# Macaron block on one core: exponentials over two PSUM banks, a shorter ring for score tiles, Q and K rows read by group

## The reference

```
x = x + 0.5 * ffn(layernorm(x))
x = x + attention(layernorm(x))
x = x + 0.5 * ffn(layernorm(x))

ffn(z):       probs = softmax(z @ router_w)                 # 8 experts, top 2 kept
              routed = sum_e combine[n, e] * (silu(z @ w1[e]) @ w2[e])
              shared = sigmoid(z @ shared_gate_w) * ((silu(gate) * up) @ shared_down)
attention(z): q, k, v = z @ Wq.T, z @ Wk.T, z @ Wv.T        # 16 heads of 8
              scores = q k^T / sqrt(8) - slope_h * (key - query), causal
              out = softmax(scores) v;  result = out @ Wo.T
```

## Time and profile before

| | |
|---|---|
| median of 3 runs | 333.55 us (333.43 to 335.55) |
| the profiled execution | 334.14 us |
| its span, first to last instruction | 331.5 us |
| TensorE busy | 287.5 us |
| VectorE busy | 253.2 us |
| ScalarE busy | 171.6 us |
| GpSimd busy | 124.5 us |
| mean granted TensorE clock | 0.958 |

### The profile page before, as it was taken

How to read it: one execution, slowest core, us unless ns; L and a number is a source line. 1 busy time by engine, 2 the same in 40 slices (tenths; PEclk the granted TensorE clock), 3 DMA queues, 4 the chain that set the end, 5 groups by cost and what they waited for, 6 DMA issues and landing times.

```text
span 331.5 us, 7083 instructions
## 1 busy us (share of the span) xinstructions
PE 287.5 (87%) x2328; PEld 186.1 (56%) x2328; DVE 253.2 (76%) x1061; ACT 171.6 (52%) x326; POOL 124.5 (38%) x253
## 2 busy tenths in 40 slices
PE   0498998989982899999899995998999999999995
PEld 0487887977650534334343343332344698889894
DVE  4559798788995488898788983899822397987865
ACT  2143332432350478877688874778688532424330
POOL 0466245306151044447414533384733342430300
PEclk9999999999996559999999998999899999999999
DMA  6810000690269002114702293000000000100010
GB/s 182 211 24 0 2 0 5 209 168 5 68 175 141 0 2 91 65 43 86 113 2 98 98 147 48 1 4 4 1 3 1 2 2 0 34 1 32 3 32 32
DMA packets 19899, 17.71 MB, mean 53 GB/s; under 512 B 1692, under 2 KB 18652, under 8 KB 19804
## 3 DMA queue, kind: packets, MB, share of 16 engines
q1 hardware_dynamic: 19144, 17.04, 23.3%
q10 hardware_dynamic: 720, 0.23, 0.3%
HBM read 9.74 MB, written 7.34 MB: 52 GB/s over the span
## 4 chain that ended last, share of the span: by engine, by line
PE 53%; DVE 16%; DMA 8%; POOL 7%; issue 6%; ACT 5%; SPq 4%; DVEq 0%; ACTq 0%; POOLq 0%
PE bank L837 13%; PE bank L968 8%; PE bank L936 7%; PE bank L775 6%; DMA QA<-smaxT 5%; DVE X L634 5%; PE bank L776 5%; PE bank L777 5%; DVE masked_s L702 3%; POOL probs L369 2%; ACT probs L479 2%; DVE stats L571 2%; DMA X<-in_x 2%; SPq L254 2%; PE bank L991 2%
## 5 line engine op out<-in xcount | busy, mean ns | idle before, releaser
L702 DVE CUSTOM_DVE_ANT_0 masked_s<-bank,causal_sb 128x512 f32<-128x512 f32 (+3 forms) x256 | 109.7, 485 | 23.9 <-PE bank L909 23.9
L479 ACT ACTIVATE probs<-bank 128x512 f32<-128x512 f32 x160 | 89.6, 602 | 39.5 <-PE bank L936 38.9
L634 DVE SCALAR_TENSOR_TENSOR X<-bank,coef,X 128x128 f32<-128x128 f32 x288 | 80.7, 342 | 21.0 <-PE bank L837 14.6
L837 PEld LDWEIGHTS bank<-w_sb,act 128*128 128x128 f32 x512 | 67.7, 193 | 5.9
L369 POOL TENSOR_SCALAR_AFFINE_SELECT probs<-probs 128x512 f32<-128x512 f32 x64 | 39.8, 636 | 79.5 <-ACT probs L479 79.5
L936 PE MATMUL bank<-QA,KA 57*128 57x128 bf16 (+3 forms) x256 | 59.3, 318 | 10.1 <-DMA QA<-smaxT 9.8
L837 PE MATMUL bank<-w_sb,act 128*128 128x128 f32 x512 | 67.9, 276 | 0.0
L909 PE MATMUL bank<-KA,QA 54*128 54x512 bf16 (+3 forms) x256 | 59.6, 320 | 6.9 <-DVE smax L702 6.0
L418 ACT ACTIVATE act<-bank 128x512 f32<-128x512 f32 x72 | 41.8, 594 | 40.1 <-PE bank L777 40.1
L968 PE MATMUL bank<-probs,VA 128*32 128x256 f32 (+2 forms) x640 | 53.4, 402 | 1.4 <-issue 0.9
L775 PE MATMUL bank<-XH,w_hi 128*128 128x512 f32 x88 | 42.8, 486 | 4.9 <-DVE gated L619 2.3
(11 more groups left out here) (83 smaller groups left out, 322.5 us busy)
## 6 DMA issues: line engine op xcount, KB each, us to landing
qk_scratch<-qk_parts SPq DMA_DIRECT2D x8, 384.0 KB, 2.6
QA<-qk_scratch SPq DMA_DIRECT2D x8, 384.0 KB, 6.1
KA<-qk_scratch SPq DMA_DIRECT2D x8, 384.0 KB, 9.5
qk_scratch<-qk_parts SPq DMA_DIRECT2D x8, 256.0 KB, 2.9
qk_scratch<-qk_parts SPq DMA_DIRECT2D x8, 128.0 KB, 2.8
QA<-smaxT SPq DMA_DIRECT2D x64, 3.0 KB
out_x<-X SPq DMA_DIRECT2D x4, 256.0 KB, 2.3
X<-in_x SPq DMA_DIRECT2D x3, 256.0 KB, 6.1
```

The source lines that it names most:

```text
L479: nc.scalar.activation(dst, src, ACT.Exp).then_inc(exp_done, 1)
L634: m = nc.vector.scalar_tensor_tensor(X[:, b * NT + t, :], Y_BANK[i % 3][:, t * P:(t + 1) * P], coef[:, j % 2, t, n:n + 1], X[:, b * NT + t ...
L702: r = nc.vector.tensor_tensor_reduce(masked_s[:, u % 4, off:off + n], bank[:, off:off + n], causal_sb[:, S - n:S], 1.0, -3e38, ALU.add, AL ...
L837: m = nc.tensor.matmul(Y_BANK[i % 3][:, r], a, w2_sb[:, n, :], start=True, stop=True)
```

## The change

Exponentials: banks 0 and 1 form one tensor (`wide0`), banks 3 and 4 another (`wide1`). Transposed units take four banks in turn, two for each pair of units; one ScalarE instruction handles a pair of units (1024 columns), once both are there, and TensorE waits at the first unit of a pair for the pair before the last. All counts of `exp_done` become counts of pairs.

Scores: bank 0 goes to the transposed units, so that score units keep the two banks 2 and 7 throughout, and TensorE waits for the scan of unit u-2.

Reads: `read_rows` takes a group in place of a batch, four DMAs of 96 KB. Those of batch 0 are issued at once as before. Those of batch 1 no longer stand ahead of `maximum_rows(0)`; group `n + 4` is read in step `n`, behind `maximum_rows(n + 1)`. TensorE waits for a group's rows at its first score unit.

```diff
--- before.py
+++ after.py
@@ -83,9 +83,14 @@
 
         scratch = nc.dram_tensor("qk_scratch", [2, B, P, 6, S], bf16, kind="Internal").ap()
 
-        banks = [ctx.enter_context(nc.psum_tensor(f"bank{i}", [P, S], f32)) for i in range(8)]
+        def psum(i, n):
+            return ctx.enter_context(nc.psum_tensor(f"bank{i}", [P, n * S], f32))
+
+        wide0, bank2, wide1 = psum(0, 2), psum(2, 1), psum(3, 2)
+        halves_of = lambda wide: [wide[:, k * S:(k + 1) * S] for k in range(2)]
+        banks = halves_of(wide0) + [bank2] + halves_of(wide1) + [psum(i, 1) for i in range(5, 8)]
         H_BANK, Y_BANK, M0, M1 = banks[0:2], banks[3:6], banks[6], banks[7]
-        T_BANK, O_BANK, MISC = [banks[3], banks[4], banks[1]], banks[5], banks[6]
+        T_BANK, T_WIDE, O_BANK, MISC = [banks[3], banks[4], banks[0], banks[1]], [wide1, wide0], banks[5], banks[6]
         ld_x = [sem(f"ld_x{b}") for b in range(B)]
@@ -108,7 +113,7 @@
         mid_qk, parts_ready = sem("mid_qk"), sem("parts_ready")
         v_ready, v_sb = sem("v_ready"), sem("v_sb")
         scr_q, scr_k = sem("scr_q"), sem("scr_k")
-        qa_ready, ka_ready = [sem("qa_ready0"), sem("qa_ready1")], [sem("ka_ready0"), sem("ka_ready1")]
+        rows_ready = [[sem(f"rows_ready{i}_{g}") for g in range(NG)] for i in range(2)]
         aot_ready, at_sb, wo_ready, x_att = sem("aot_ready"), sem("at_sb"), sem("wo_ready"), sem("x_att")
 
         s_ready, s_used = sem("s_ready"), sem("s_used")
@@ -142,7 +147,7 @@
 
         def score_bank(u):
 
-            return banks[(2, 7)[u % 2]] if u < EARLY else banks[(2, 7, 0)[(u - EARLY) % 3]]
+            return banks[(2, 7)[u % 2]]
 
         def early_scores(n):
 
@@ -180,7 +185,7 @@
 
         STEPS = range(0, NGT + 1)
         QK_SCALE = (float(HD) ** -0.5, 1.0)
-        XT_AT, READ_AT = {0: 2, 5: 3}, {4: 2, 8: 3}
+        XT_AT, VALUES_AT = {0: 2, 5: 3}, {4: 2, 8: 3}
 
         def projected_at(n, phase):
 
@@ -234,16 +239,18 @@
                     sp.dma_start(dst[:, 3:5, :], part[:, 0:2, :]).then_inc(scr_k, 16)
                     sp.dma_start(dst[:, 5, :], part[:, 0, :]).then_inc(scr_k, 16)
 
-            def read_rows(b):
-
+            def read_rows(G):
+
+                b, g = divmod(G, NG)
                 if b >= 2:
-                    sp.wait_ge(t_ready, NU * NG * (b - 1))
-                for i, (scr, to, ready) in enumerate(((scr_q, QA, qa_ready), (scr_k, KA, ka_ready))):
+                    sp.wait_ge(t_ready, NU * (G - 2 * NG + 1))
+                pairs = slice(GH // 2 * g, GH // 2 * (g + 1))
+                for i, (scr, to) in enumerate(((scr_q, QA), (scr_k, KA))):
                     sp.wait_ge(scr, 48 * (b + 1))
                     rows = scratch[i, b].rearrange("(pair par d) s n -> par d s pair n", par=2, d=HD)
                     for par in range(2):
-                        sp.dma_start(to[b % 2][64 * par:64 * par + PROD, :, :],
-                                     rows[par].rearrange("d s pair n -> (d s) pair n")).then_inc(ready[b % 2], 16)
+                        sp.dma_start(to[b % 2][64 * par:64 * par + PROD, pairs, :],
+                                     rows[par][:, :, pairs, :].rearrange("d s pair n -> (d s) pair n")).then_inc(rows_ready[b % 2][g], 16)
 
             def maximum_rows(G):
 
@@ -257,13 +264,15 @@
             for b in range(2):
                 write_parts(b, 0)
                 write_parts(b, 1)
-                read_rows(b)
+                if b == 0:
+                    for G in range(NG):
+                        read_rows(G)
             maximum_rows(0)
             for n in STEPS:
                 if 0 <= n + 1 < NGT:
                     maximum_rows(n + 1)
-                if n in READ_AT:
-                    read_rows(READ_AT[n])
+                if n + NG < NGT:
+                    read_rows(n + NG)
                 if (b := projected_at(n, 2)) is not None:
                     write_parts(b, 0)
                 if (b := projected_at(n, 3)) is not None:
@@ -363,7 +372,7 @@
 
             def mask(G, tiles):
                 for kt, need in tiles:
-                    pool.wait_ge(exp_done, NU * G + need)
+                    pool.wait_ge(exp_done, NU // 2 * G + need)
                     blk = probs[G % 2][:, :, POS[kt]:POS[kt] + P]
 
                     nc.gpsimd.affine_select(out=blk, in_=blk, compare_op=ALU.is_ge, fill=0.0, base=0,
@@ -372,12 +381,12 @@
             ffn(0)
             for n in STEPS:
                 if 0 <= n < NGT:
-                    mask(n, ((0, 4), (3, 8), (1, 8)))
+                    mask(n, ((0, 2), (3, 4), (1, 4)))
                 for k in range(2):
                     if (b := projected_at(n, 2 + k)) is not None:
                         low_qk(b, k)
                 if 0 <= n < NGT:
-                    mask(n, ((2, 10),))
+                    mask(n, ((2, 5),))
                 if 0 <= n + 2 < NGT:
                     split_smax(n + 2)
                 if n == LAST_LN:
@@ -462,20 +471,19 @@
                 nc.scalar.activation(VA[b % 2][:, :, :, 0:HD],
                                      M0[:, :].rearrange("p (t h d) -> p t h d", t=NT, d=HD), ACT.Copy).then_inc(v_sb, 1)
 
-            def exps(G, i):
-                u = NU * G + i
-                ac.wait_ge(t_ready, u + 1)
-                if i == 0 and G >= 2:
+            def exps(G, k):
+                u = NU // 2 * G + k
+                ac.wait_ge(t_ready, 2 * u + 2)
+                if k == 0 and G >= 2:
                     ac.wait_ge(pv_ready, G - 1)
-                a = prob_units(G % NG)[i]
-                head = a[0][1] - GH * (G % NG)
-                bank = T_BANK[u % 3]
-                if a[0][2] == 2:
-                    dst = probs[G % 2][:, head:head + 3:2, POS[2]:POS[2] + 2 * P]
-                    src = bank[:, :].rearrange("p (h n) -> p h n", h=2)
+                kt, src = prob_units(G % NG)[2 * k][0][2], T_WIDE[u % 2]
+                if kt == 2:
+                    dst = probs[G % 2][:, :, POS[2]:POS[2] + 2 * P].rearrange("p (h i) n -> p i h n", i=2)
+                    src = src[:, :].rearrange("p (i h n) -> p i h n", i=2, h=2)
                 else:
-                    pos = POS[a[0][2]]
-                    dst, src = probs[G % 2][:, head, pos:pos + S], bank[:, :]
+                    head = 2 * (k % 2)
+                    dst = probs[G % 2][:, head:head + 2, POS[kt]:POS[kt] + S]
+                    src = src[:, :].rearrange("p (i n) -> p i n", i=2)
                 nc.scalar.activation(dst, src, ACT.Exp).then_inc(exp_done, 1)
 
             def copy_smax(G):
@@ -517,8 +525,8 @@
             load_table(1, ACT.Exp)
             for n in STEPS:
                 for i in range(NU):
-                    if 0 <= n < NGT:
-                        exps(n, i)
+                    if 0 <= n < NGT and i % 2:
+                        exps(n, i // 2)
                     if (n, i) in VALUE_SLOTS:
                         values(VALUE_SLOTS.index((n, i)))
                     if i == 3 and 0 <= n + 1 < NGT:
...
@@ -894,13 +902,10 @@
                 if u == 0:
                     pe.wait_ge(ld_ac, 16 * 10)
                     pe.wait_ge(shift_ready, B)
-                if 2 <= u < EARLY + 2:
+                if u >= 2:
                     pe.wait_ge(s_used, u - 1)
-                elif u > EARLY + 2:
-                    pe.wait_ge(s_used, u - 2)
-                if i == 0 and g == 0:
-                    pe.wait_ge(qa_ready[b % 2], 32 * (b // 2 + 1))
-                    pe.wait_ge(ka_ready[b % 2], 32 * (b // 2 + 1))
+                if i == 0:
+                    pe.wait_ge(rows_ready[b % 2][g], 64 * (b // 2 + 1))
                 a, dst = score_units(g)[i], score_bank(u)
                 for k, (off, h, qt) in enumerate(a):
                     lo = 64 * (h % 2)
@@ -927,13 +932,13 @@
                 u = NU * G + i
                 if i == 0:
                     pe.wait_ge(nm_rows[G % 2], 64 * (G // 2 + 1))
-                if u >= 3:
-                    pe.wait_ge(exp_done, u - 2)
+                if i % 2 == 0 and u >= 4:
+                    pe.wait_ge(exp_done, u // 2 - 1)
                 a = prob_units(g)[i]
                 for k, (off, h, kt) in enumerate(a):
                     lo = 64 * (h % 2)
                     r = slice(lo, lo + ROWS_T)
-                    m = nc.tensor.matmul(T_BANK[u % 3][:, off:off + WID[kt]], KA[b % 2][r, h // 2, kt * P:(kt + 1) * P],
+                    m = nc.tensor.matmul(T_BANK[u % 4][:, off:off + WID[kt]], KA[b % 2][r, h // 2, kt * P:(kt + 1) * P],
                                          QA[b % 2][r, h // 2, kt * P:S], start=True, stop=True, skip_group_check=True)
                     if k == len(a) - 1:
                         m.then_inc(t_ready, 1)
...
@@ -1035,7 +1040,7 @@
                         pe.wait_ge(s_used, NU * NGT)
                         logits(B, ln_index(2, 0))
                     if n == NGT and i in (0, 4):
-                        pe.wait_ge(exp_done, NU * NGT)
```

(1 more changed line is left out.)

8 lines of the change are left out of this document (4 added, 4 removed).

## The result

| | before | after |
|---|---|---|
| median, same chip | 334.55 us (4 runs) | **341.77 us** (4 runs, 339.95 to 345.09) |
| ratio | | 1.0192, interval 1.0113 to 1.0271 |
| profiled execution, its span | 334.14, 331.5 us | 341.82, 339.7 us |
| TensorE, VectorE, ScalarE busy | 287.5, 253.2, 171.6 us | 297.6, 255.3, 163.8 us |

The account below looks back on a forecast made before the run. It saw TensorE and VectorE nearly balanced in ordinary steps, with two long TensorE gaps for maximum rows. Terms -11.4 + 10.3 + 0.85 gave -0.25 us, so 333.3 us was forecast, no change that can be told, range 327 to 339.

Parts of the forecast that it names:

- the term for exponentials of two tiles: Attention steps: later ends of paired exponentials cost 0.85 us, 0.4 at step 5's end and 0.45 at the last step's.
- The ring: Score tiles from step 0 on: two banks make TensorE wait for the scan two tiles earlier, costing 10.3 us.
- the reads: Sync queue order: earlier maximum rows gain 6.1 us before step 0, 3.8 before step 10 and 1.5 of clock, 11.4 together.
- the later start computed above: Ordinary steps: score tiles start later behind scans with two banks, hiding the pairs' later ends within 0.1 us; nothing charged.
- Two places have no cover: Step 5's end, TensorE waiting for the transposed input's split, 0.4 us; last step's end, first hidden matmul, 0.45 us.
- the prediction's own sign of being wrong: Changed profile: other clock falls than before, or step starts moving by less than the waits in front of them.
- The third term: Step 10: it ran at 0.82 of the clock after the gap, 1.7 us lost; 1.5 us taken as gained.
- Rival 4: Sync queue: reads by group collide with the maximum rows, 1 us in each of 12 steps, 345 us; chance 0.05.
- The middles of steps: Score tile 6 waits for tile 4's scan, 0.39 us later, in nine steps (3, 4, 5, 8 to 13).
- The first: Step starts: longer scan waits with two banks bring four more clock falls of about 1.5 us, 339 us; chance 0.20.
- Rival 2: Attention steps: slack hides waits of the two-bank score ring, leaving 6.6 us of them, 329 us; chance 0.24.
- Rival 3: Steps 0 and 1: the clock stays up or returns sooner, 6.8 us at most, 326.4 us; chance 0.10.

Follow-up runs that it names:

- single exponentials: The changed kernel with one exponential per transposed tile in place of pairs, its four banks for transposed tiles kept: 333.41 us, ratio 0.9941 to the kernel before.
- reads alone: The kernel before with only Q and K rows read by group in the new sync queue order: 324.38 us, ratio 0.9684.
- the old reads: The changed kernel with rows read a batch at a time, as in the kernel before: 347.81 us, ratio 1.0391 to the kernel before.
- the kernel kept busy: The kernel before with reads by group, plus 12 unused matmuls between its last early score tiles: four executions, 319.94, 319.96, 325.26 and 325.57 us.
- the kernel with pairs 0 and 3: The changed kernel with wide exponentials only for pairs 0 and 3 of each step's five, the others tile by tile: 333.44 us.

## Why the prediction was wrong

**What failed: the term for exponentials of two tiles.** It had 0.85 us, and 8.4 were measured: 7.5 of the 8.5 us between the forecast of 333.3 and the result. (The ring was 1.3 cheaper than forecast, the reads 0.2 weaker, and the kernel before 1.0 slower beside the kernel after than in the forecast. The 1.0 that is left is the kernel before again, another 1.0 slower in the set in which the parts were timed.) The step that failed is this: "In an ordinary step this runs beside the later start computed above, within 0.1 us, so I charge nothing. Two places have no cover." The 0.4 us by which a pair ends later were right (0.43). So were the two places: TensorE's wait for the split at the end of step 5 grew by 0.33 (forecast 0.4), that at the last step's end by 0.42 (forecast 0.45), from the first to the second of these rows, single exponentials and after:

```profile
256.93 0.51 PE L779 MATMUL bank<-XH,w_hi 128*128 128x512 f32 x1 [0.69 <-ACT probs L483]
```

```profile
263.54 0.75 PE L783 MATMUL bank<-XH,w_hi 128*128 128x512 f32 x1 [1.11 <-ACT probs L487]
```

(The lower end given for a pair's own time, 0.96, left out the second one's end: two queued exponentials take 0.48 + 0.60 = 1.08, and the pair took 1.02.) But the count of places was wrong. The prediction named who waits for the pair and stopped at ScalarE's copy of the maxima; it did not ask who waits for that copy. TensorE does, through bank 6, wherever a projection or a transpose follows. By the distances between tiles that is 0.43 in four steps for pair 1, 0.43 in four for pair 2, and 0.31 to 0.42 at four places for pair 4: **4.8 us**. The later start computed for ordinary steps does not cover them: step 7 has such a later start (0.97 us from its first transposed tile to the second, with pairs and without, and 0.22 before), and with pairs it still pays its two waits of 0.43 in full.

The other half, in the profiled executions, is **the clock**, for which the sum had no term beyond the falls of before; the prediction's own sign of being wrong, "a clock column with other falls than before", came true. Kernel after, windows in steps 4 and 6 and behind the last step:

```profile
147.00:151.00 4.00, 3.92 (x27) 1.08 (x25) 2.89 (x10) 2.18 (x3) 3.61 (x8) 0.57 0.13 37
168.00:171.00 3.00, 3.00 (x15) 1.95 (x14) 1.31 (x4) 2.00 (x3) 0.00 (x0) 0.51 0.00 0
...
264.00:267.00 3.00, 3.00 (x20) 0.99 (x18) 1.10 (x5) 2.07 (x4) 0.22 (x2) 0.50 0.02 5
```

The kernel with single exponentials has none of these three falls. They cost 1.3 us in step 4 (11.56 against 10.22), 1.3 in step 6 (2.17 less two waits of 0.43), and about 1.5 behind the last step (the 2.15 us by which the rest is longer, less 0.42 and 0.24 of waits). With 0.7 less in step 1, where the clock came back sooner, and a start 0.5 earlier, the sum is 4.8 + 0.2 + 4.1 - 0.7 - 0.5 = 7.9, against 8.1 between the two spans. This split holds for the two profiled executions. The execution of the kernel after with the highest mean clock, 0.960, still took 339.95 us, 6.5 above the 333.4 of single exponentials, which have 0.958 to 0.963 in nine of ten executions. So the clock may be less than half of the 8.4 us.

**The reads, right.** Forecast 11.4 us; measured 11.2 alone. Start 5.9 (6.1), step 9's wait 4.0 (3.8), step 10 1.3 (1.5). That these three make the same 11.2 as the medians is luck: 2.1 were given back, most of it in steps 0 and 11, and the medians have 2.1 from outside the spans and from the kernel before's clock. The third term was right by size and wrong by reason, since step 11 paid it back: the fall was not avoided but came later. Rival 4 did not happen; a read by group lands in 2.3 us and no wait for maximum rows over 1 us is left. Step 9 lasts 8.28 us (forecast 8.5).

**The ring, right.** Forecast 10.3; measured 9.0. Step by step, between reads alone and single exponentials: step 0 1.0 (1.7), step 1 3.2 (2.2), 2 0.1 (0.2), 3 and 4 1.4 (1.4), 5 0.6 (0.6), 6 0.0 (0), 7 0.6 (0.4), 8 0.8 (0.8), 9 0.6 (0.6), 10 and 11 1.0 (1.0), 12 and 13 -0.2 (1.4; the kernel with reads alone had a fall of the clock in step 13). The sum is helped by two errors of opposite sign, both of the clock: step 1 has 1.0 too much, with the long stretch ending at 122.3 us in place of 117.6, and steps 12 and 13 have 1.6 too little. The middles of steps came out exactly: in all nine steps that were named, the distance from transposed tile 6 to 7 is 1.50 us in place of 1.11, the forecast 0.39. The method, holding each tile against the scan two tiles earlier, can be seen at work in step 8 of the kernel after:

```profile
190.12 0.42 DVE L710 CUSTOM_DVE_ANT_0 masked_s<-bank,causal_sb 128x256 f32<-128x256 f32 x1
...
190.60 0.39 PE L914 MATMUL bank<-KA,QA 54*128 54x512 bf16 x1 [0.37 <-DVE smax L710]
```

```profile
194.54 0.55 DVE L710 CUSTOM_DVE_ANT_0 masked_s<-bank,causal_sb 128x384 f32<-128x384 f32 x1
...
195.16 0.23 PE L914 MATMUL bank<-KA,QA 54*128 54x128 bf16 x1 [0.17 <-DVE smax L710]
```

The scans end at 190.54 and 195.09, and score tiles 0 and 6 start 0.06 and 0.07 us later, where tile 6 was forecast to the hundredth.

**The loader's wait.** The prediction did not count the 21.8 us of the earlier trace rows, and rightly. In the kernel after this wait, from 102 to 257 us, has gone to

```profile
PEld bank L941 <- ACT probs L487: 2.7, 6, 0.8
```

and no gain of time came with it.

**The rivals.** The first, slower by falls of the clock, came nearest with 339. Falls did take part of the loss, but not by the cause it named: behind the long stretch the short ring without pairs has one fall (two with the old reads), where the kernel before has two. The rule cited from the Trainium skill ("TensorE: Matmul & The Clock Gate", section "A second HAM failure mode: psum-queue depth-cycling") is borne out in part: with the pairs, which lengthen the pauses at banks, four falls stand behind the start against one without them. The short ring by itself speaks against it, since its longer pauses went with one fall in place of the two with reads alone. Rival 2 fell: the waits of the short ring were not hidden. Rival 3 fell as well, and its price was too high: the kernel kept busy gives 3.4 us back in steps 0 and 1, not 6.8.

**What stays open.** Why the clock falls at one pause and not at a like one, and whether the pairs bring the falls at all: the kernel with pairs 0 and 3 has the fall of step 6 and is as fast as the one with none. The kernel that is fastest here, with no pairs, also has a fall in step 4 (11.32 us), and two of its four executions have a lower mean clock still. So the 4.1 us of the profiled execution are tied to the pairs by counts (mean clocks 0.958 to 0.963 in nineteen of the twenty executions of the two kernels at 333.4, 0.934 to 0.960 after), and not by a mechanism that a run isolates.

## What to carry to other kernels

When an instruction is made to end later, follow its engine's queue behind it to the end: each instruction there that frees a bank is a wait for whoever fills that bank next, even when nobody waits for the instruction itself. Batching on an engine with slack bought nothing here and delayed all of its followers; the batches without such a follower were free, and the other three cost 8.4 us. Take one part of a bundled change at a time: one of the three parts was worth 11 us, and the other two gave back 17.
